# Softmax attention layer on one core: two positions of the tensor engine's order taken together

## The chip, the cores and the metric

One core of one Trainium2 chip runs the whole program in one launch. The metric is device time in microseconds (us). The core's engines are TensorE (PE in the profile; PEld is its weight load), VectorE (DVE), ScalarE (ACT), GpSimd (POOL) and SyncE (SP), which here only issues transfers. Each engine runs its own instructions in the order in which the program lists them and waits at semaphores for the others.

## The reference

Four stages follow each other, each with a residual and a layer norm: a causal softmax attention with a projection (8 batches of 1024 tokens, width 256, 16 heads of 16) and a small linear layer behind it, a linear attention with a feed-forward layer, and a mixture of experts. The change touches the first alone:

```python
att = jnp.einsum('bhqd,bhkd->bhqk', q, k) * SCALE      # q, k, v: 8 x 16 x 1024 x 16
att = jnp.where(causal, att, -jnp.inf)
att = jax.nn.softmax(att, axis=-1)
y = jnp.einsum('bhqk,bhkd->bhqd', att, v)
y = y.transpose(0, 2, 1, 3).reshape(B, T, C)
return y @ W_proj + b_proj
```

## The kernel before, in words

`softmax_layer` (from line 293) computes the first stage. A batch is walked in 48 **positions** k: 4 groups of 4 heads, and 12 pieces of the causal triangle in each (`SEGS`). At a position TensorE does this, for each of two `pair`s of heads:

- `scores(k, pair)`, called S below (line 774): the transposed scores of 128 keys against up to 512 queries, the row maxima already subtracted by two extra rows of the operand. ScalarE's `exponentials` (line 880) turns them into `probs`.
- `maxima(k + 16, pair)`, called M (line 760): plain scores of a piece that is due 16 positions later (`LM`), only to find the maxima. VectorE's `reduce` (lines 1034 and 1037) reads them.

Besides, a position has `values(k - 2)`, called V (line 794, both pairs at once: probabilities by values into `psum_o`), and at most one **unit**, called U: a transposition, a projection or part of one, from the table `UNIT_AT` (positions 1 to 44 have one). Names of units: T1, QK and V prepare the next batch; YT, P, T2, F and END finish the one before; OUT transposes attended heads; N transposes the maxima (line 733).

The widths of S, M and V go with k modulo 12. S and M of a position have 512 columns at 0 and 4 to 8, 384 at 1 and 9, 256 at 2 and 10, 128 at 3 and 11. V has the width of position k - 2.

What sets the order:

- S and M share a ring of three places in PSUM, `R` (tile `a_scores`): S(k,0), M(k,0), S(k,1), M(k,1), S(k+1,0) and so on. A product may start when the third before it has been taken out. So each S waits for VectorE's reduction of the M two products ahead of that, and each M for ScalarE's exponential of an S: M(k,1) for that of S(k,0), M(k+1,0) for that of S(k,1), S(k+1,0) for the reduction of M(k,0), S(k+1,1) for that of M(k,1).
- All units share one single place, `G` (tile `a_general`), which ScalarE or VectorE empties in `take`, at the start of the next position. The next unit waits for that.
- V(k) waits for the exponentials of position k, and where the causal edge cuts, for GpSimd's `cut`. VectorE's `copy_out` (line 1062) takes `psum_o` out at k modulo 12 = 1 and 5, behind a V.
- VectorE also does statistics (`BATCH_NORM_STATS2`, lines 1120 and 1128), the combination of maxima `together` (line 1045) at k = 8, 20, 32, 44, and `minus` (lines 1053 and 1056), which takes out N.
- SyncE's part and GpSimd's part are lists of their own, untouched.

The order of TensorE at one position is that of `turn` in `of_tensor` (line 805):

```python
scores(b, RU, k, 0)
maxima(b + (k + LM) // NK, b, RU, k + LM, 0)      # if more
values(b, RU, k - 2)
scores(b, RU, k, 1)
maxima(b + (k + LM) // NK, b, RU, k + LM, 1)      # if more
unit(batch_of(b, UNIT_AT[k]), b, U, UNIT_AT[k])   # if there is one
```

Of the kernel before, what the change touches and what calls it, by code (L numbers as in the profile page):

```python
# [292 lines left out]
def softmax_layer(nc, ctx, ident, minus_half, spot, x_rows, W_qkv, b_qkv, W_proj, b_proj, weight,  # L293
# [14 lines left out]
    NK = HG * NSEG  # L308
# [3 lines left out]
    LM = 16  # L312
# [185 lines left out]
    def kept(what, with_head, with_tail):  # L498
        if what[0] in TAIL_UNITS:
            return with_tail  # L500
        return with_head or not (what[0] in HEAD_UNITS or what == ("N", 4))
# [4 lines left out]

    def r_units(u0, with_head):
        units = {}
        for k in range(NK):
            for pair in range(2):  # L510
                units["S", k, pair] = u0 + len(units)
                if k + LM < NK or with_head:
                    units["M", k + LM, pair] = u0 + len(units)
        return units

    H_SEQ = ([("T1", i) for i in range(4)] + [("QK", i) for i in range(4)] +
# [11 lines left out]
    RU_TURN = r_units(2 * LM, True)  # L528
# [149 lines left out]
    def of_tensor(pe, prepare):  # L678
# [121 lines left out]
        def batch_of(b, what):  # L800
            if what[0] in TAIL_UNITS:
                return b - 1
            return b + 1 if what[0] in HEAD_UNITS or what == ("N", 4) else b

        def turn(b, U, RU, with_head, with_tail, prepare=None):
            for k in range(NK):
                more = k + LM < NK or with_head
                scores(b, RU, k, 0)
                if more:
                    maxima(b + (k + LM) // NK, b, RU, k + LM, 0)  # L810
                if k > 1:
                    values(b, RU, k - 2)
                elif with_tail:
                    values(b - 1, RU_TURN, NK - 2 + k)
                scores(b, RU, k, 1)
                if more:
                    maxima(b + (k + LM) // NK, b, RU, k + LM, 1)
                if k in UNIT_AT and kept(UNIT_AT[k], with_head, with_tail):
                    unit(batch_of(b, UNIT_AT[k]), b, U, UNIT_AT[k])

        def before():
            for what in H_SEQ[0:12]:
# [23 lines left out]
    def of_scalar(act, prepare):  # L846
# [52 lines left out]
        def turn(b, U, RU, with_head, with_tail, prepare=None):  # L899
            for k in range(NK):  # L900
                what = UNIT_AT.get(k - 1)
                if what and what[0] in ON_ACT and kept(what, with_head, with_tail):
                    take(b - 1 if what[0] in TAIL_UNITS else b + 1, b, U, what)
                exponentials(b, RU, k, 0)
                exponentials(b, RU, k, 1)
                if with_head and k in HEAD_APPLY:
                    head_apply(b + 1, HEAD_APPLY[k])
                if with_tail and k in TAIL_APPLY:
                    tail_apply(b - 1, *TAIL_APPLY[k])
# [112 lines left out]
    def of_vector(dve, prepare):  # L1022
# [112 lines left out]
        def turn(b, U, RU, with_head, with_tail, prepare=None):  # L1135
            for k in range(NK):
                n, mk = k % NSEG, k + LM
                more = mk < NK or with_head
                what = UNIT_AT.get(k - 1)
                if what and what[0] in ON_DVE and kept(what, with_head, with_tail):  # L1140
                    of = (b - 1 if what[0] in TAIL_UNITS else
                          b + 1 if what[0] in HEAD_UNITS or what == ("N", 4) else b)
                    take(of, b, U, what)
                if more:
                    reduce(b, b, RU, mk, 0)
                if n == 5:
                    copy_out(b, k // NSEG * 2)
                elif n == 1 and k > 1:
                    copy_out(b, k // NSEG * 2 - 1)
                elif k == 1 and with_tail:  # L1150
                    copy_out(b - 1, 2 * HG - 1)
                if n == 8 and (mk - 1 < NK or with_head):
                    together((mk - 1) // NSEG, b, RU, mk - 1)
                if with_head and k == HEAD_SUM:
                    ln_h.sum_first(dve, b + 1, chain_h)
                if with_head and k == HEAD_SUM + 1:
                    ln_h.sum_third(dve, b + 1, chain_h)
                if with_tail and k in TAIL_SUM:
                    ln_t.sum_first(dve, b - 1, chain_t)
                if with_tail and k - 1 in TAIL_SUM:  # L1160
                    ln_t.sum_third(dve, b - 1, chain_t)
                if more:
                    reduce(b, b, RU, mk, 1)
                if with_head and k in HEAD_STATS:
                    head_statistics(b + 1, HEAD_STATS[k])
                if with_head and k == HEAD_SUM:
                    ln_h.sum_second(dve, b + 1, chain_h)
                if with_tail and k in TAIL_STATS:
                    tail_statistics(b - 1, b, U, TAIL_STATS[k][0], TAIL_STATS[k][1:])
                if with_tail and k in TAIL_SUM:  # L1170
                    ln_t.sum_second(dve, b - 1, chain_t)
                if prepare is not None:
                    prepare(k)
# [1805 lines left out]
```

How the kernel before makes its waits and increments, by code:

```python
    def wait_free(self, eng, b, u):  # L76
        eng.wait_ge(self.evacuated[u % self.slots], b * self.per + self.start + u // self.slots)
# [1 line left out]
    def wait_full(self, eng, b, u):  # L79
        eng.wait_ge(self.full[u % self.slots], b * self.per + u // self.slots + 1)
# [1 line left out]
    def wait_evacuated(self, eng, b, u):  # L82
        eng.wait_ge(self.evacuated[u % self.slots], b * self.per + self.start + u // self.slots + 1)
# [1 line left out]
    def wait_evacuated_before(self, eng, b, u):  # L85
        eng.wait_ge(self.evacuated[u % self.slots], b * self.per + u // self.slots + 2)
# [12 lines left out]
    def link(self, eng, b, ins):  # L100
        self.at += 1
        ins.then_inc(self.sem, 1)
        eng.wait_ge(self.sem, b * self.per + self.at)
# [5 lines left out]
    def wait(self, eng, b):  # L109
        eng.wait_ge(self.sem, b * self.per + self.at)
# [74 lines left out]
            @block.gpsimd  # L185
            def _(pool):
                nc.gpsimd.memset(ident[:, :], 0.0).then_inc(made, 1)
                nc.gpsimd.memset(minus_half[:, :], -0.5).then_inc(made, 1)
                pool.wait_ge(made, 2)
                nc.gpsimd.affine_select(out=ident[:, :], in_=ident[:, :], compare_op=ALU.not_equal,
                                        fill=1.0, base=0, pattern=[[-1, P]],
                                        channel_multiplier=1).then_inc(made, 1)
                pool.wait_ge(made, 3)
                nc.gpsimd.iota(number[:, :], [[P, G4]], base=0, channel_multiplier=1
                               ).then_inc(made, 1)
# [470 lines left out]
        def wait_scores():  # L666
            sp.wait_ge(pv_done, B * NK + PV0)
```

## Time and profile before

| what | value |
|---|---|
| median of 3 runs | 4210.25 us (4207.5 to 4215.37) |
| the profiled execution's own time | 4209.16 us |
| its span, first to last instruction | 4207.4 us |
| busy in the span: PE, DVE, ACT, POOL | 93%, 64%, 50%, 28% |
| the stage of the change | from 103.6 us (first S) to 1325.3 us (last S) |

The profile is one execution. A row of the view of instructions in time gives start, duration, engine, source line, operation, what is written and read, and how many were merged; in brackets the idle time of the engine before it and what ended that. Durations of matmuls are longer than the distance between starts, since they overlap: S with 512 columns is shown with 0.50 us, and the next product starts 0.34 us later. The argument goes by starts.

### The profile page before, as it was taken

To read this page: it belongs to the slowest core of one execution; us is meant where nothing else is said; L and a number is where in the kernel's file an instruction comes from. 1 tells how busy PE (TensorE), PEld (TensorE's weight loads), DVE (VectorE), ACT (ScalarE), POOL (GpSimd) and SP (SyncE) were. 2 spreads that over 40 slices of the span, in tenths; PEclk is the share of its full clock that TensorE was granted. 3 is DMA by queue.
4 is the path that set the end of the run, shared out by engine and by line. 5 is a ranking of instruction groups with operands and counts; after the bars stand their busy time and mean duration, and the time that the engine had idled before them with its cause. 6 is when DMAs were issued, how large, how long until landed. Compare 5 with 4: busy or idle time off the path is not lost. (4 is left out here: it accounts for less than half of the span.)

```text
span 4207.4 us, 74610 instructions
## 1 busy us (share of the span) xinstructions
PE 3893.2 (93%) x28676; PEld 3028.3 (72%) x28676; DVE 2712.3 (64%) x7778; ACT 2115.5 (50%) x3994; POOL 1172.9 (28%) x1083
## 2 busy tenths in 40 slices
PE   4999999999999899999999999999999599999993
PEld 2444444444545788888888888888888499999992
DVE  5888888888785565555565565555555555555555
ACT  1566666666666555554455554554454333333333
POOL 3233343343333211111112111111111133333335
PEclk8899999999988999999999999999999799999996
DMA  3543544443441100000000000000001133333345
GB/s 70 99 97 57 97 92 67 87 98 61 77 110 43 36 26 21 22 21 21 20 22 22 22 19 19 16 20 10 20 20 34 52 65 65 73 69 65 65 122 173
DMA packets 177203, 230.73 MB, mean 55 GB/s; under 512 B 27388, under 2 KB 152411, under 8 KB 176848
## 3 DMA queue, kind: packets, MB, share of 16 engines
q1 hardware_dynamic: 148816, 189.53, 19.6%
q0 software_dynamic: 25728, 28.03, 4.5%
q10 hardware_dynamic: 2304, 8.39, 0.5%
q8 instruction: 228, 3.74, 0.4%
q14 instruction: 127, 1.04, 0.1%
HBM read 94.30 MB, written 87.05 MB: 43 GB/s over the span
## 5 line engine op out<-in xcount | busy, mean ns | idle before, releaser
L880 ACT ACTIVATE probs<-a_scores 128x1024 f32<-128x1024 f32 (+3 forms) x768 | 615.7, 811 | 337.7 <-PE a_scores L774 331.8
L1034 DVE CUSTOM_DVE_ANT_0 a_scores<-a_scores,mask 128x384 f32<-128x384 f32 (+3 forms) x1024 | 480.6, 514 | 101.9 <-PE a_scores L760 96.2
L774 PEld LDWEIGHTS a_scores<-q_st,k_st 50*128 50x128 f32 x1536 | 149.1, 191 | 355.4 <-issue 201.5
L273 POOL TENSOR_TENSOR l_ln_rstd<-l_ln_ve,minus_half 128x4 f32<-128x4 f32 x80 | 82.0, 1025 | 1047.5 <-DVE l_ln_ve L246 1047.1
L1842 ACT ACTIVATE l_o<-l_num,l_den 128x64 f32<-128x64 f32 x960 | 222.0, 319 | 292.6 <-DVE l_den L2328 281.1
L774 PE MATMUL a_scores<-q_st,k_st 50*128 50x512 f32 (+3 forms) x1536 | 349.9, 453 | 10.3 <-DVE mx L1034 4.0
L760 PE MATMUL a_scores<-k_st,q_st 48*128 48x512 f32 (+3 forms) x1536 | 305.9, 396 | 50.7 <-ACT probs L880 22.1
L1037 DVE TENSOR_REDUCE mx<-a_scores 128x2 f32<-128x1024 f32 x256 | 309.9, 1221 | 60.8 <-PE a_scores L760 60.1
L794 PE MATMUL a_out<-probs,v_aug 128*32 128x512 f32 (+3 forms) x3072 | 345.1, 523 | 3.4 <-POOL probs L961 3.2
L961 POOL TENSOR_SCALAR_AFFINE_SELECT probs<-probs 128x512 f32<-128x512 f32 x256 | 164.8, 645 | 518.5 <-ACT probs L880 507.3
L2664 PE MATMUL e_out<-e_weights_hi,e_hT_hi 128*128 128x256 f32 x1088 | 303.8, 279 | 0.0
L2664 PE MATMUL e_out<-e_weights_hi,e_hT_lo 128*128 128x256 f32 x1088 | 303.8, 279 | 0.0
L2664 PE MATMUL e_out<-e_weights_lo,e_hT_hi 128*128 128x256 f32 x1088 | 303.7, 279 | 0.0
L2711 ACT ACTIVATE e_to_split<-e_hidden,e_b 128x384 f32<-128x384 f32 (+1 forms) x320 | 200.0, 625 | 196.9 <-PE e_hidden L2649 189.8
L1751 PE MATMUL l_num<-l_v,l_scores_kept 128*128 128x65 f32 x2048 | 286.2, 263 | 0.0
L1751 PEld LDWEIGHTS l_num<-l_v,l_scores_kept 128*128 128x128 f32 x2048 | 271.2, 193 | 0.0
L1856 ACT ACTIVATE l_o<-l_general 128x512 f32<-128x512 f32 x256 | 152.6, 596 | 218.1 <-PE l_general L1600 199.0
L2733 POOL DMA_INDIRECT expert_sums_scratch<-e_y,e_number x136 | 221.6, 1629 | 69.6 <-issue 37.2
L2229 DVE TENSOR_TENSOR l_a<-l_general,l_a 128x512 f32<-128x512 f32 x64 | 44.3, 692 | 299.6 <-PE l_general L1559 161.2
L760 PEld LDWEIGHTS a_scores<-k_st,q_st 48*128 48x128 f32 x1536 | 154.4, 198 | 114.5 <-ACT probs L880 80.7
L2649 PE MATMUL e_hidden<-e_rT_hi,e_weights_hi 128*128 128x384 f32 (+1 forms) x640 | 233.8, 365 | 0.0
L1746 PE MATMUL l_num<-l_state,l_qT 128*128 128x130 f32 x1024 | 231.6, 308 | 0.0
(294 smaller groups left out, 10569.4 us busy)
## 6 DMA issues: line engine op xcount, KB each, us to landing
q_st<-parts SPq DMA_DIRECT2D x192, 128.0 KB, 4.5
k_st<-parts SPq DMA_DIRECT2D x192, 128.0 KB, 6.8
expert_rows_scratch<-empty_row SPq DMA_DIRECT2D x34, 520.0 KB, 9.5
l_x<-x_scratch SPq DMA_DIRECT2D x32, 512.0 KB, 3.8
e_weights<-in_L_ffn_W_dram SPq DMA_DIRECT2D x16, 1024.0 KB, 7.3
e_rows<-expert_rows_scratch SPq DMA_DIRECT2D x24, 390.0 KB
e_rows<-expert_rows_scratch SPq DMA_DIRECT2D x16, 520.0 KB
x_in<-in_L_attn_x_dram SPq DMA_DIRECT2D x8, 1024.0 KB, 5.5
```

The lines of the kernel that those rows point to most:

```text
L760: last = nc.tensor.matmul(psum_r[:, R.slot(u), h2, 0:w], q_st[rows, 2 * hg + pair, j * P:(j + 1) * P], k_st[rows, 2 * hg + pair, k0:k1], s ...
L774: last = nc.tensor.matmul(psum_r[:, R.slot(u), h2, 0:w], k_st[rows, 2 * hg + pair, i * P:(i + 1) * P], q_st[rows, 2 * hg + pair, q0:q0 + w ...
L794: last = nc.tensor.matmul(psum_o[32 * h4:32 * h4 + 32, q0 - half * HALF:HALF], v_aug[:, i, h * DV0:h * DV0 + 32], probs[:, k % 3, h4, 0:w] ...
L880: nc.scalar.activation(probs[:, k % 3, 2 * pair:2 * pair + 2, 0:w], psum_r[:, R.slot(u), :, 0:w], ACT.Exp).then_inc(R.evacuated[R.slot(u)], 1)
L1034: last = nc.vector.tensor_tensor_reduce(s, s, mask[:, HALF - w:HALF], 1.0, LEAST, ALU.add, ALU.max, out[:, h2, :])
L1037: last = nc.vector.tensor_reduce(out.rearrange("p h a -> p (h a)"), psum_r[:, R.slot(u), :, 0:w], AX.X, ALU.max)
L1746: nc.tensor.matmul(psum_n[:, NUM.slot(n), p2 * 2 * DV:(p2 + 1) * 2 * DV], qT[:, p, j * P:(j + 1) * P], state[:, p, :], start=True, stop=Fa ...
L1751: last = nc.tensor.matmul(psum_n[:, NUM.slot(n), h4 * DV:(h4 + 1) * DV], scores[:, d % 2, h2, p % 4, :], v_aug[:, j, 4 * g4 + h4, :], star ...
L1842: last = nc.scalar.activation(o[:, j % 2, head:head + DH1], psum_n[:, NUM.slot(n), h * DV:h * DV + DH1], ACT.Copy, scale=den[:, n % 2, 1, ...
L2649: last = nc.tensor.matmul(psum_h[:, HU.slot(u), 0:n * P], w1[a][:, e2, c, m * P:(m + 1) * P], rT[b][:, q % 2, c, 0:n * P], start=(k == 0), ...
L2664: last = nc.tensor.matmul(psum_y[:, s, (j - 2 * s) * D:(j - 2 * s + 1) * D], hT[a][:, q % 2, m, j * P:(j + 1) * P], w2[b][:, e2, m, :], st ...
L2733: nc.gpsimd.indirect_dma_start(out=sums_dram, out_offset=bass.IndirectOffsetOnAxis(ap=number[:, q % RING, j:j + 1], axis=0), in_=y[:, q % ...
```

## The change

Positions are taken two at a time, k even. TensorE's order for a pair of positions becomes

- S(k,0) M(k,0) S(k,1) V(k-2) M(k,1)
- S(k+1,0) M(k+1,0) U(k) V(k-1) S(k+1,1) M(k+1,1) U(k+1)

The unit of an even position moves behind the first S and M of the odd one, beside V. ScalarE and VectorE follow: at an odd position the first exponential and the first reduction now stand ahead of the `take` of the even position's unit. `r_units` is rewritten, but numbers the ring as before. No instruction is added or removed, and GpSimd's and SyncE's lists stay.

```diff
@@ turn in of_tensor
-            for k in range(NK):
-                more = k + LM < NK or with_head
+            for k in range(0, NK, 2):
+                more, of = k + LM < NK or with_head, b + (k + LM) // NK
                 scores(b, RU, k, 0)
                 if more:
-                    maxima(b + (k + LM) // NK, b, RU, k + LM, 0)
+                    maxima(of, b, RU, k + LM, 0)
+                scores(b, RU, k, 1)
                 if k > 1:
                     values(b, RU, k - 2)
                 elif with_tail:
-                    values(b - 1, RU_TURN, NK - 2 + k)
-                scores(b, RU, k, 1)
+                    values(b - 1, RU_TURN, NK - 2)
                 if more:
-                    maxima(b + (k + LM) // NK, b, RU, k + LM, 1)
+                    maxima(of, b, RU, k + LM, 1)
+                scores(b, RU, k + 1, 0)
+                if more:
+                    maxima(of, b, RU, k + 1 + LM, 0)
                 if k in UNIT_AT and kept(UNIT_AT[k], with_head, with_tail):
                     unit(batch_of(b, UNIT_AT[k]), b, U, UNIT_AT[k])
+                if k > 1:
+                    values(b, RU, k - 1)
+                elif with_tail:
+                    values(b - 1, RU_TURN, NK - 1)
+                scores(b, RU, k + 1, 1)
+                if more:
+                    maxima(of, b, RU, k + 1 + LM, 1)
+                if k + 1 in UNIT_AT and kept(UNIT_AT[k + 1], with_head, with_tail):
+                    unit(batch_of(b, UNIT_AT[k + 1]), b, U, UNIT_AT[k + 1])
@@ turn in of_scalar
                 what = UNIT_AT.get(k - 1)
+                if k % 2 == 1:
+                    exponentials(b, RU, k, 0)
                 if what and what[0] in ON_ACT and kept(what, with_head, with_tail):
                     take(b - 1 if what[0] in TAIL_UNITS else b + 1, b, U, what)
-                exponentials(b, RU, k, 0)
+                if k % 2 == 0:
+                    exponentials(b, RU, k, 0)
                 exponentials(b, RU, k, 1)
@@ turn in of_vector
                 what = UNIT_AT.get(k - 1)
+                if k % 2 == 1 and more:
+                    reduce(b, b, RU, mk, 0)
                 if what and what[0] in ON_DVE and kept(what, with_head, with_tail):
...
                     take(of, b, U, what)
-                if more:
+                if k % 2 == 0 and more:
                     reduce(b, b, RU, mk, 0)
```

TensorE at positions 6 and 7 of a batch that has a batch before it (L774 is S, L760 is M, L794 is V, L692 a unit P, L681 a unit YT). Before:

```order
L681 MATMUL a_general<-ident,y_att 128x128 x4
L774 MATMUL a_scores<-q_st,k_st 128x512 x2
L760 MATMUL a_scores<-k_st,q_st 128x512 x2
L794 MATMUL a_out<-probs,v_aug 32x512 x4
L774 MATMUL a_scores<-q_st,k_st 128x512 x2
L760 MATMUL a_scores<-k_st,q_st 128x512 x2
L692 MATMUL a_general<-w_proj,yT 128x256 x4
L774 MATMUL a_scores<-q_st,k_st 128x512 x2
L760 MATMUL a_scores<-k_st,q_st 128x512 x2
L794 MATMUL a_out<-probs,v_aug 32x512 x4
```

The same place in the changed kernel (L776 is S, L762 M, L796 V, L694 P, L683 YT):

```order
L683 MATMUL a_general<-ident,y_att 128x128 x4
L776 MATMUL a_scores<-q_st,k_st 128x512 x2
L762 MATMUL a_scores<-k_st,q_st 128x512 x2
L776 MATMUL a_scores<-q_st,k_st 128x512 x2
L796 MATMUL a_out<-probs,v_aug 32x512 x4
L762 MATMUL a_scores<-k_st,q_st 128x512 x2
L776 MATMUL a_scores<-q_st,k_st 128x512 x2
L762 MATMUL a_scores<-k_st,q_st 128x512 x2
L694 MATMUL a_general<-w_proj,yT 128x256 x4
L796 MATMUL a_out<-probs,v_aug 32x512 x4
```

V(4) went from ahead of S(6,1) to behind it, and the unit of position 6 from behind M(6,1) to behind M(7,0).

VectorE from the second reduction of position 8 on (each masked reduction is a row with the product's width and a short one that reads its result; L1120 are statistics, L1053 and L1056 take out the unit N of position 8). Before:

```order
L1034 ISA a_scores,mx<-a_scores,mask 128x512
L1034 ISA mx 128x1
L1120 BN_STATS a_ln_tail_stats<-att 128x6 x2
L1053 TENSOR_SCALAR nm_hi<-a_general 32x128
L1056 SCALAR_TENSOR_TENSOR nm_lo<-a_general,nm_hi 32x128
L1034 ISA a_scores,mx<-a_scores,mask 128x384
L1034 ISA mx 128x1
```

In the changed kernel:

```order
L1051 ISA a_scores,mx<-a_scores,mask 128x512
L1051 ISA mx 128x1
L1137 BN_STATS a_ln_tail_stats<-att 128x6 x2
L1051 ISA a_scores,mx<-a_scores,mask 128x384
L1051 ISA mx 128x1
L1051 ISA a_scores,mx<-a_scores,mask 128x384
L1051 ISA mx 128x1
L1070 TENSOR_SCALAR nm_hi<-a_general 32x128
L1073 SCALAR_TENSOR_TENSOR nm_lo<-a_general,nm_hi 32x128
```

The reduction of M(9,0), two halves of 384 columns, went ahead of the two instructions that take out N.

## Rows read from the trace of the kernel before

**Rows 1.** The page: busy time of each engine, and two of its lines in 40 slices.

```profile
PE 3893.2 (93%) x28676; PEld 3028.3 (72%) x28676; DVE 2712.3 (64%) x7778; ACT 2115.5 (50%) x3994; POOL 1172.9 (28%) x1083
...
PE   4999999999999899999999999999999599999993
...
DVE  5888888888785565555565565555555555555555
```

**Rows 2.** Windows of one batch: us, busy PE, PEld, DVE, ACT, POOL, PEclk, DMA share, GB/s.

```profile
407.00:560.00 153.00, 145.22 (x1014) 72.93 (x1014) 132.34 (x396) 103.83 (x152) 59.86 (x68) 1.00 0.44 83
```

**Rows 3.** One source line, L1053: it runs four times in a batch.

```profile
L1053 DVE TENSOR_SCALAR nm_hi<-a_general x32: 260/273/275, 99.2 to 1289.2; 32x128 fp32r<-32x128 f32 x32
```

**Rows 4.** Waits from 100 to 1200 us: total us, times, longest.

```profile
PE a_scores L760 <- ACT probs L880: 19.6, 49, 0.7
...
PE a_general L733 <- DVE mx L1045: 11.5, 14, 1.0
```

**Rows 5.** Groups by shape in one batch (560 to 714 us): busy us, mean ns | idle before.

```profile
L880 ACT ACTIVATE probs<-a_scores 128x1024 f32<-128x1024 f32 x48 | 48.8, 1024 | 14.9 <-PE a_scores L774 14.3
L1037 DVE TENSOR_REDUCE mx<-a_scores 128x2 f32<-128x1024 f32 x32 | 38.7, 1220 | 6.0 <-PE a_scores L760 6.0
```

**Rows 6.** TensorE in time, second half of position 5 and position 6 of batch 3.

```profile
573.87 0.50 PE L774 MATMUL a_scores<-q_st,k_st 50*128 50x512 f32 x2
574.42 0.49 PE L760 MATMUL a_scores<-k_st,q_st 48*128 48x512 f32 x2
574.84 0.66 PE L681 MATMUL a_general<-ident,y_att 128*128 128x128 f32 x4
575.43 0.50 PE L774 MATMUL a_scores<-q_st,k_st 50*128 50x512 f32 x2
575.77 0.39 PE L760 MATMUL a_scores<-k_st,q_st 48*128 48x512 f32 x2
576.09 1.06 PE L794 MATMUL a_out<-probs,v_aug 128*32 128x512 f32 x8
577.08 0.50 PE L774 MATMUL a_scores<-q_st,k_st 50*128 50x512 f32 x2
577.42 0.39 PE L760 MATMUL a_scores<-k_st,q_st 48*128 48x512 f32 x2
```

**Rows 7.** VectorE in time, then ScalarE, the same stretch.

```profile
575.18 0.68 DVE L1062 COPY oT<-a_out 128x512 f32<-128x512 f32 x1
575.78 1.22 DVE L1037 TENSOR_REDUCE mx<-a_scores 128x2 f32<-128x1024 f32 x1
...
576.03 1.02 ACT L880 ACTIVATE probs<-a_scores 128x1024 f32<-128x1024 f32 x1
```

**Rows 8.** VectorE in time around the taking out of N, positions 8 and 9.

```profile
587.76 0.74 DVE L1120 BATCH_NORM_STATS2 a_ln_tail_stats<-att 128x6 f32<-128x256 f32 x2
588.43 0.26 DVE L1053 TENSOR_SCALAR nm_hi<-a_general 32x128 fp32r<-32x128 f32 x1
588.72 0.28 DVE L1056 SCALAR_TENSOR_TENSOR nm_lo<-a_general,nm_hi 32x128 fp32r<-32x128 f32 x1
588.93 0.54 DVE L1034 CUSTOM_DVE_ANT_0 a_scores<-a_scores,mask 128x384 f32<-128x384 f32 x1
...
589.92 0.59 DVE L1034 CUSTOM_DVE_ANT_0 a_scores<-a_scores,mask 128x384 f32<-128x384 f32 x1
```

**Rows 9.** TensorE in time: the unit of position 9 and the product ahead of it.

```profile
588.84 0.34 PE L760 MATMUL a_scores<-k_st,q_st 48*128 48x384 f32 x2
589.11 0.70 PE L692 MATMUL a_general<-w_proj,yT 128*128 128x256 f32 x2
```

**Rows 10.** The same at positions 20 and 21: TensorE's units, and VectorE's second instruction on N.

```profile
627.46 0.41 PE L733 MATMUL a_general<-ident,mx 128*32 128x128 f32 x2 [0.94 <-DVE mx L1045]
...
629.54 0.28 DVE L1056 SCALAR_TENSOR_TENSOR nm_lo<-a_general,nm_hi 32x128 fp32r<-32x128 f32 x1
...
629.88 0.50 PE L740 MATMUL a_general<-xnT_hi,w_qkv_hi 128*128 128x512 f32 x1
```

More of the change, by code:

```diff
@@ L508, in r_units @@
         units = {}
-        for k in range(NK):
[L510 to L513, printed above, removed]
+        for k in range(0, NK, 2):
+            more = k + LM < NK or with_head
+            for at in (k, k + 1):
+                for pair in range(2):
+                    units["S", at, pair] = u0 + len(units)
+                    if more:
+                        units["M", at + LM, pair] = u0 + len(units)
         return units
@@ L805, in turn @@
         def turn(b, U, RU, with_head, with_tail, prepare=None):
-            for k in range(NK):
-                more = k + LM < NK or with_head
+            for k in range(0, NK, 2):
+                more, of = k + LM < NK or with_head, b + (k + LM) // NK
                 scores(b, RU, k, 0)
                 if more:
-                    maxima(b + (k + LM) // NK, b, RU, k + LM, 0)
+                    maxima(of, b, RU, k + LM, 0)
+                scores(b, RU, k, 1)
                 if k > 1:
@@ L813, in turn @@
                 elif with_tail:
-                    values(b - 1, RU_TURN, NK - 2 + k)
-                scores(b, RU, k, 1)
+                    values(b - 1, RU_TURN, NK - 2)
                 if more:
-                    maxima(b + (k + LM) // NK, b, RU, k + LM, 1)
+                    maxima(of, b, RU, k + LM, 1)
+                scores(b, RU, k + 1, 0)
+                if more:
+                    maxima(of, b, RU, k + 1 + LM, 0)
                 if k in UNIT_AT and kept(UNIT_AT[k], with_head, with_tail):
                     unit(batch_of(b, UNIT_AT[k]), b, U, UNIT_AT[k])
+                if k > 1:
[3 more added lines that the diff above has]
+                scores(b, RU, k + 1, 1)
+                if more:
+                    maxima(of, b, RU, k + 1 + LM, 1)
+                if k + 1 in UNIT_AT and kept(UNIT_AT[k + 1], with_head, with_tail):
+                    unit(batch_of(b, UNIT_AT[k + 1]), b, U, UNIT_AT[k + 1])
         def before():
```

## The prediction

> **What bounds the kernel now.** I read the page first: TensorE is busy 93% of the span and in tenths of 9 almost everywhere, VectorE 8 tenths only in the first third, which is the stage of the change [rows 1]. Everything outside that stage keeps its instructions and order, so the change is worth what it does to the 8 batches. Their length comes from a line that runs four times a batch: 31 intervals from 99.2 to 1289.2 us, so (1289.2 - 99.2) / 31 x 4 = 153.5 us a batch [rows 3]. The window of one batch shows TensorE 145.2 of 153 us busy, VectorE 132.3, ScalarE 103.8, at a granted clock of 1.00 [rows 2]. So TensorE has at most some 8 us of idle in a batch by the records, and VectorE has 20 us of slack, 13%: it is close enough behind to decide wherever its work is not spread evenly.
>
> The waits say where TensorE's idle is. M waits for exponentials (19.6 us) and the unit N for VectorE's combined maxima (11.5 us), in 1100 us, which are 7.2 batches: 2.7 and 1.6 us a batch [rows 4].
>
> **Prices, from starts.** S to M takes 0.34 us, M to V 0.32, a V of 512 columns 0.99, S to M again 0.34 [rows 6]. A full exponential takes 1.02 and a full reduction 1.22 [rows 5]. The reduction of M(5,1), started on TensorE at 574.42, ran from 575.78 to 577.00, because the copy of `psum_o` (575.18) went first; S(6,1), which needs its place, started at 577.08 [rows 6, 7].
>
> **What the change leaves alone.** No engine gets more work, the ring's numbering is the same, and SP's and POOL's lists stay, so no transfer is passed by anything. Only distances move. Before, every S and M had a V or a unit on either side: the lead of each hand-over was nearly the same. Now there are runs S M S and M S M without anything between, and runs with V and U together.
>
> **Part 1, gain: the M behind exponentials.** At an odd position M(k,1) waited for the exponential of S(k,0), which stood behind ScalarE's taking out of a unit. S(5,1) to M(5,1) took 0.55 instead of 0.34 [rows 6]: 0.21 lost. Now this exponential goes first and a unit lies in between, so it goes. Seven odd positions have this form. But M(k+1,0) now comes after S M S V M S and needs both exponentials of the even position. Behind a unit that ScalarE takes out they begin 0.60 after S(k,0), as at position 6 (576.03 - 575.43), and end at 0.60 + 2 x 1.02 = 2.64 [rows 6, 7]. With a V of 256 columns (some 0.57) the TensorE work is 0.34 + 0.32 + 0.34 + 0.57 + 0.32 + 0.34 = 2.23: a new wait of 0.4. So part of the gain is given back at the even positions with a narrow V. Ends: nothing, and all of the 2.7 us a batch [rows 4]. I take 1.1 us a batch, nearer to the lower end because the give-back is seen to be of the size of the gain.
>
> **Part 2, loss: V behind an S that waits for VectorE.** At even k, S(k,1) needs the reduction of M(k-1,1). Before, V(k-2) lay between and was done while VectorE finished. At position 6 V(4) ran from 576.09 to 577.08, and the reduction ended at 577.00: the wait cost nothing [rows 6, 7]. In the new order TensorE comes to S(6,1) at 576.09, waits until 577.05 and only then does V(4): M(6,1) can start at 577.05 + 0.34 + 0.99 = 578.4, before 577.42. That is 1.0 us. Nor is the reduction earlier: at position 5 the copy waits for V(3), which now stands behind unit 4. The form needs a light unit or none at k-1 (a heavy one, such as P, covers the wait); that is k = 2, 6, 14, 30 with the copy ahead of the reduction, and 0, 32, 34, 44, 46 without. Walking the starts of these stretches in the same way gives 0.8 for positions 0 to 3, 1.2 for 4 to 7, 0.6 for 12 to 17, 0.3 for 28 to 31, nothing sure for 44 to 47: 2.9 us a batch. In 12 to 17 this already holds the gain of part 1. Ends: 0 and twice as much.
>
> **Part 3, loss: the unit's single place.** A unit of an even position is now followed by the next one after only V S M, and VectorE takes it out one reduction later. At position 8 VectorE has no idle ahead of it: statistics 587.76, N taken out 588.43 to 589.00, and unit 9 starts at 589.11, right at the end of the M before it (588.84 + 0.27) [rows 8, 9]. Now two halves of 384 columns go first; from 588.93 to 589.92 they take 0.99 us [rows 8]. N's place is free at 590.0, and unit 9 waits for it 0.9 us. At position 21 the same: taken out at 629.54 + 0.28 = 629.82, unit at 629.88 [rows 10], so another 1.0. Here the gain of the later N is contained: N waited 0.94 for the maxima [rows 10] and now waits less, but the next unit is held by the later taking out. Position 33 by the same walk 0.4; position 39, a QK behind OUT with a reduction of 128 columns and statistics ahead of it, 0.7. Together 3.0 us a batch. Ends: 0, if VectorE is earlier there for another reason, and 4.5.
>
> **The sum.** 2.9 + 3.0 - 1.1 = 4.8 us a batch. The first and the last batch lack part of the units, so I count 7: 34 us. On the profiled execution's own time of 4209.2 this is 4243; the median of the runs shown is 1 us higher and nothing else. The granted clock was 1.00 in the middle batches [rows 2], and I count no change of it.
>
> **The rivals.** *Faster: the waits for exponentials and maxima go and VectorE's slack pays for the rest.* The Trainium skill (same page, Optimization Strategy) advises one to find the gaps of the chosen engine and let what ends them start sooner; this change does that for TensorE. If it holds, half of the 19.6 us (the odd positions) and the 11.5 us go [rows 4]: 4209 - 21 = 4188. For it: the waits are real, and VectorE has 13% slack. Against: at 575.78 and 587.76 VectorE runs without idle just where the new order asks more of it. It decides if reductions at even positions end before the second S comes.
>
> *No change.* What one pair loses, the next regains, since later waits are shortened by VectorE having caught up: within 8 us of 4210. For it: the total of work is the same. Against: the stalls are followed by positions that had no wait to give back (10, 11).
>
> *Much slower.* The late reductions pile up: each holds the next exponentials and S too, and more of the units with a single place are held. Then the upper ends of parts 2 and 3 hold and nothing is gained: (5.8 + 4.5) x 7 = 72, so 4281. Against: VectorE's load of 87% lets it catch up at positions of 128 and 256 columns, and where ScalarE takes a unit out, V, S and M (0.99 + 0.34 + 0.32 = 1.65 us) mostly cover that [rows 6]. The Trainium skill has a rule on this side (Perfetto Trace Analysis, Optimizing Tensor Performance, Matmuls): groups of matmuls should rotate through different PSUM banks, so that taking one out lies beside the next. By that rule each of some 20 odd units would be held; at 0.9 each (an estimate with unit 9's price) that would be 126 us and a time of 4335. The trace of before bears it out for VectorE's units only.
>
> *The change does not do what it says* is no case: the order above shows it done on three engines.
>
> **How the numbers follow.** A measurement tells about 0.2%, 8.4 us, from no change. My forecast (a loss of 12 to 55 us around 4243) has 0.60, faster 0.15, no change 0.14, much slower 0.11. All of the first and the last are slower by over 0.2%, and one in seven of the no-change case (0.02) could fall out above: slower 0.73, same 0.12, faster 0.15. The range takes in my forecast, the no-change case and a part of the faster one, and on the other side all but the full pile-up: 4194 to 4270. That leaves out some 0.1 on either side.
>
> **What would show it.** In the new profile a batch, by the same line's 31 intervals, should be 158.3 us instead of 153.5; waits of L776 (S) for VectorE's maxima should have grown, waits of L762 (M) for exponentials should have fallen to half or less; the units of positions 9 and 21 should wait for the second instruction on N by some 0.9 us; and V(4) should start after S(6,1). I am wrong if the batch is 153 us or less, or if the time is lost at M behind exponentials instead.

## The result, and the profile after

The changed kernel takes 4291.7 us (median of 4 runs, 4283.0 to 4309.8) against 4208.9 of the kernel before beside it: a ratio of 1.0204, 95% interval 1.0182 to 1.0226. It is 83 us slower; 34 were forecast, and the time lies above the range. The profiled execution has a span of 4281.3 us.

The page of the changed kernel, as [rows 1], with the line of the granted clock:

```profile
PE 3918.0 (92%) x28676; PEld 3051.8 (71%) x28676; DVE 2699.9 (63%) x7778; ACT 2105.4 (49%) x3994; POOL 1172.1 (27%) x1083
...
PEclk8889999899898999999999999999999799999996
```

The work is that of before: instruction counts and busy times of VectorE, ScalarE and GpSimd hardly move. TensorE's busy time rises by 25 us with the same 28676 matmuls, so some took longer in the records. The line that runs four times a batch, as [rows 3]:

```profile
L1070 DVE TENSOR_SCALAR nm_hi<-a_general x32: 273/274/279, 102.1 to 1363.3; 32x128 fp32r<-32x128 f32 x32
```

(1363.3 - 102.1) / 31 x 4 = 162.7 us a batch: 9.2 more than before, 71 us in the 31 intervals. So the loss is in this stage, as expected. Windows of the changed kernel, columns as in [rows 2]: one as long as that of before, one at positions 2 and 3 of batch 3, one from position 46 of batch 3 to position 3 of batch 4.

```profile
407.00:560.00 153.00, 139.54 (x958) 71.36 (x958) 123.24 (x375) 97.47 (x146) 55.59 (x64) 0.96 0.45 84
595.00:604.00 9.00, 8.10 (x45) 3.94 (x46) 5.50 (x26) 3.14 (x7) 2.91 (x4) 0.62 0.97 186
750.00:768.00 18.00, 17.77 (x98) 7.82 (x98) 11.05 (x44) 9.15 (x15) 6.71 (x8) 0.53 0.86 148
```

The granted clock is 0.96 where it was 1.00, and the fall lies in short stretches that come back in each batch, in which it is close to 0.50: the level of 1.2 GHz instead of 2.4. There a value product of 512 columns takes almost twice as long. TensorE at positions 2 and 3 of batch 3, changed kernel (start, duration, and in brackets the idle time before and what ended it):

```profile
596.49 0.49 PE L776 MATMUL a_scores<-q_st,k_st 50*128 50x256 f32 x2 [0.90 <-DVE mxb L1051]
596.92 1.93 PE L796 MATMUL a_out<-probs,v_aug 128*32 128x512 f32 x8
598.78 0.58 PE L762 MATMUL a_scores<-k_st,q_st 48*128 48x256 f32 x2
```

V(0) takes 598.78 - 596.92 = 1.86 us from start to start instead of 0.99 [rows 6]. Ahead of it stands the wait that part 2 of the forecast describes.

At position 6 that part can be read as forecast: S(6,1) waits for VectorE, and V(4) starts behind it.

```profile
608.85 0.49 PE L776 MATMUL a_scores<-q_st,k_st 50*128 50x512 f32 x2
609.22 0.50 PE L762 MATMUL a_scores<-k_st,q_st 48*128 48x512 f32 x2
610.33 0.50 PE L776 MATMUL a_scores<-q_st,k_st 50*128 50x512 f32 x2 [0.60 <-DVE mx L1054]
610.76 1.06 PE L796 MATMUL a_out<-probs,v_aug 128*32 128x512 f32 x8
611.76 0.50 PE L762 MATMUL a_scores<-k_st,q_st 48*128 48x512 f32 x2
```

The reduction it waits for, and the copy ahead of that, as [rows 7]:

```profile
608.46 0.68 DVE L1079 COPY oT<-a_out 128x512 f32<-128x512 f32 x1
609.05 1.22 DVE L1054 TENSOR_REDUCE mx<-a_scores 128x2 f32<-128x1024 f32 x1
```

It ends at 610.27, and S(6,1) starts at 610.33. From S(6,0) to M(6,1) are 2.91 us; before they were 1.99 [rows 6]. At positions 8 and 9 part 3 can be read. VectorE's taking out of N, and the unit of position 9, as [rows 8, 9]:

```profile
622.70 0.55 DVE L1051 CUSTOM_DVE_ANT_0 a_scores<-a_scores,mask 128x384 f32<-128x384 f32 x1
...
623.99 0.28 DVE L1073 SCALAR_TENSOR_TENSOR nm_lo<-a_general,nm_hi 32x128 fp32r<-32x128 f32 x1
```

```profile
622.62 0.35 PE L762 MATMUL a_scores<-k_st,q_st 48*128 48x384 f32 x2
624.32 0.91 PE L694 MATMUL a_general<-w_proj,yT 128*128 128x256 f32 x3 [1.35 <-DVE nm_lo L1073]
```

TensorE idles 1.35 us for the second instruction on N; 0.9 was worked out. Waits of TensorE in the same 1100 us as [rows 4]:

```profile
PE a_scores L776 <- DVE mx L1054: 12.3, 29, 0.7
PE a_scores L776 <- DVE mxb L1051: 10.4, 25, 0.9
...
PE a_scores L776 <- DVE mx L1051: 8.6, 18, 0.8
PE a_general L742 <- DVE nm_lo L1073: 8.5, 7, 1.3
PE a_general L694 <- DVE nm_lo L1073: 8.2, 6, 1.4
PE a_scores L762 <- ACT probs L894: 7.7, 24, 0.7
...
PE a_general L735 <- DVE mx L1062: 0.2, 1, 0.2
```

The two waits at which the change aims did fall: M behind exponentials from 19.6 to 7.7 us, N behind the maxima from 11.5 to 0.2 [rows 4]. Two others grew. S behind reductions takes 31 us. In the kernel before it was 6, in the same view:

```profile
PE a_scores L774 <- DVE mx L1034: 3.7, 10, 1.1
...
PE a_scores L774 <- DVE mxb L1034: 1.6, 6, 0.5
...
PE a_scores L774 <- DVE mx L1037: 0.8, 2, 0.5
```

And the units behind VectorE's taking out of the unit before them wait some 49 us in sum, where they waited 6.

**A table by pairs.** The starts of S(k,0) show each pair of positions by itself. The table gives the mean over batches 1 to 6 from one pair's first S to the next pair's, in us, from the traces of the kernels before and after and of eight of the experiments below (their labels without e_), one execution each.

```
pair   before   after  v_only  u_only  thin_old  thin_new  fill   thin_fill  before_fill  n_first
46      4.22    5.94    4.62    4.69     4.30      4.48    6.58     5.40        4.90       4.60
 0      4.93    5.52    4.67    4.94     4.88      4.67    5.51     5.50        5.50       5.41
 2      4.72    7.76    8.12    5.30     4.72      7.24    4.92     4.92        4.56       6.20
 4      5.39    5.40    7.32    5.55     5.56      6.84    5.55     5.40        5.39       5.96
 6      8.50    9.30   10.12    9.36     9.29     10.06    9.30     8.49        8.49       9.45
 8      7.11    8.07    7.07    8.07     8.07      7.12    8.07     7.12        7.11       7.07
10      5.90    5.71    5.90    6.43     5.71      5.90    5.71     5.90        5.89       6.16
12      6.18    6.68    6.07    6.50     6.12      6.68    6.89     6.88        6.42       6.45
14      5.93    7.78    7.89    5.68     5.97      7.07    5.42     5.63        5.17       6.91
16      8.14    7.78    8.30    8.93     8.94      7.91    7.53     7.29        7.74       9.08
18      7.88    8.03    8.11    8.97     8.02      7.97    8.03     7.81        7.83       8.82
20      7.37    7.72    7.37    7.73     7.70      7.37    7.71     7.36        7.37       6.71
22      6.38    6.66    6.28    6.65     6.66      6.28    6.66     6.53        6.28       6.82
24      7.57    7.12    7.14    7.39     7.13      7.15    7.12     7.18        7.15       7.13
26      5.64    5.74    5.65    6.13     5.75      5.63    5.75     5.64        5.63       5.75
28      5.39    5.22    5.39    5.48     5.23      5.40    5.23     5.39        5.40       5.23
30      5.96    6.31    6.43    6.66     6.29      5.95    6.30     5.96        5.96       6.29
32      6.01    6.85    6.21    6.44     6.85      6.01    6.85     6.01        6.01       6.21
34      7.33    7.20    8.03    7.77     7.72      7.33    7.20     7.33        7.33       7.83
36      7.79    7.72    7.79    7.98     7.72      7.79    7.72     7.79        7.79       7.72
38      5.85    6.32    5.88    6.32     6.32      5.87    6.32     5.86        5.87       6.32
40      7.63    7.39    7.61    7.49     7.38      7.61    7.39     7.64        7.61       7.39
42      6.83    6.93    7.25    7.56     6.95      6.83    6.94     6.82        6.84       6.94
44      6.31    5.76    6.22    5.54     5.75      6.30    5.76     6.32        6.30       6.21
sum   154.96  164.90  165.42  163.53   159.00    161.46  160.43   156.17      154.53     162.67
```

Of the 9.9 us that a batch lost, 7.7 are at the pairs 46, 0, 2, 12 and 14, called thin stretches below: there the products are narrow or the units light or missing.

The means of the kernel before hold two falls of the clock of its own. Pair 24 takes 7.13 us in five of the six batches and 9.78 in batch 1; in batch 6 the pairs 12, 14 and 16 take 6.68, 8.08 and 10.10, in the other five 6.08, 5.50 and 7.75. So at pair 24 the new order (7.12) gains nothing, though the means say 0.45, and at pair 16 (7.78) neither.

### The profile page after: what moved, and what is told of

Read it like the earlier page. It is cut to its first block and busy times, and to the rows that moved or that the text cites. A ratio compares the mean times of both kernels' runs of the same rounds, so it can differ in the third digit from the quotient of the medians.

```text
span 4281.3 us, 74610 instructions
## 1 busy us (share of the span) xinstructions
PE 3918.0 (92%) x28676; PEld 3051.8 (71%) x28676; DVE 2699.9 (63%) x7778; ACT 2105.4 (49%) x3994; POOL 1172.1 (27%) x1083
## 5 line engine op out<-in xcount | busy, mean ns | idle before, releaser
L894 ACT ACTIVATE probs<-a_scores 128x1024 f32<-128x1024 f32 (+3 forms) x768 | 606.1, 811 | 396.1 <-PE a_scores L776 391.4
L796 PE MATMUL a_out<-probs,v_aug 128*32 128x512 f32 (+3 forms) x3072 | 374.0, 554 | 2.2 <-POOL probs L978 2.2
L776 PE MATMUL a_scores<-q_st,k_st 50*128 50x512 f32 (+3 forms) x1536 | 332.3, 432 | 45.3 <-DVE mxb L1051 15.0
L762 PE MATMUL a_scores<-k_st,q_st 48*128 48x512 f32 (+3 forms) x1536 | 317.2, 419 | 31.7 <-ACT probs L894 9.1
L776 PEld LDWEIGHTS a_scores<-q_st,k_st 50*128 50x128 f32 x1536 | 154.9, 199 | 263.2 <-issue 100.3
L762 PEld LDWEIGHTS a_scores<-k_st,q_st 48*128 48x128 f32 x1536 | 158.7, 203 | 229.0 <-ACT probs L894 140.2
```

Of the source, the lines that this page charges most:

```text
L762: last = nc.tensor.matmul(psum_r[:, R.slot(u), h2, 0:w], q_st[rows, 2 * hg + pair, j * P:(j + 1) * P], k_st[rows, 2 * hg + pair, k0:k1], s ...
L776: last = nc.tensor.matmul(psum_r[:, R.slot(u), h2, 0:w], k_st[rows, 2 * hg + pair, i * P:(i + 1) * P], q_st[rows, 2 * hg + pair, q0:q0 + w ...
L796: last = nc.tensor.matmul(psum_o[32 * h4:32 * h4 + 32, q0 - half * HALF:HALF], v_aug[:, i, h * DV0:h * DV0 + 32], probs[:, k % 3, h4, 0:w] ...
L894: nc.scalar.activation(probs[:, k % 3, 2 * pair:2 * pair + 2, 0:w], psum_r[:, R.slot(u), :, 0:w], ACT.Exp).then_inc(R.evacuated[R.slot(u)], 1)
```

## The experiments

Two theories stood against each other. **A**: the order makes TensorE wait in the thin stretches, the granted clock falls there, and this is most of what the forecast missed. **B or C**: the waits themselves are larger than worked out, because one place for the units (B) or late reductions (C) drag what follows; the lower clock is a by-product. The expectations call a stretch in which the granted clock is near 0.50 a half-clock stretch; below it is a low stretch.

All experiments are one kernel with sets of even positions: `V_LATE` (V behind the second S), `U_LATE` (unit in the odd position) and `TAKE_LATE` (ScalarE's and VectorE's taking behind the first exponential and reduction). All empty is the order of before, all full is the change.

```diff
+            for k in range(NK):
+                late_v = k % 2 == 0 and k in V_LATE
                 scores(b, RU, k, 0)
                 if more:
                     maxima(of, b, RU, k + LM, 0)
+                if k % 2 == 1 and k - 1 in U_LATE and has(k - 1):
+                    do_unit(k - 1)
+                if not late_v:
+                    do_values(k)
                 scores(b, RU, k, 1)
+                if late_v:
+                    do_values(k)
                 if more:
                     maxima(of, b, RU, k + LM, 1)
+                if has(k) and not (k % 2 == 0 and k in U_LATE):
+                    do_unit(k)
```

**V moved alone.**

```diff
+    V_LATE = list(range(0, 48, 2))
+    U_LATE = TAKE_LATE = []
```

> V alone is moved (behind the second S at even positions); the units and the orders of ScalarE and VectorE are those of before. Theory A (V behind an S that waits for VectorE starves TensorE in the thin stretches, positions 46 to 3 and 12 to 15, and the granted clock falls there): most of the loss is here, about +50 us against before, clock in the middle batches 0.95, pair 2-3 near 7 us instead of 4.7, pairs 8-9 and 38-39 as before (7.11 and 5.85). Theory B (the units' single place is the cause, and it drags the rest): under +15 us, clock 1.00.

Measured: ratio 1.0203 (1.0173 to 1.0234), 4294.5 us. Pair 2 takes 8.12, pair 14 7.89, pairs 8 and 38 are as before. The granted clock between 250 and 1180 us is 0.93, where the changed kernel has 0.94. The places and the clock are those of theory A, but its size is missed: 85 us over before instead of 50, so V alone costs as much as the whole change. Of the batches 2 to 5 the one with the least of the low level (batch 3, 3.4 us) takes 159.1 us, the others (20.5 to 27.3 us) 164.7 to 166.2.

**The unit moved alone**, with its taking.

```diff
+    V_LATE = []
+    U_LATE = TAKE_LATE = list(range(0, 48, 2))
```

> The unit of the even position alone is moved, with ScalarE's and VectorE's late taking; V stays where it was before. Theory A: pairs 8-9, 20-21, 32-33 and 38-39 lose 0.3 to 1.0 each, the thin stretches nothing: +10 to +20 us, clock 1.00. Theory B: +50 us or more and a clock of 0.95 in the middle batches.

Measured: ratio 1.0160 (1.0134 to 1.0186), 4279.7 us, 67 us over before. Theory A gave at most 20 and missed; the time is the one that theory B gave (50 or more), but not its clock. The clock over the same stretch is 0.98, and pair 2 takes 5.30, so this loss is mostly not the clock's: batches 1 and 5 have no low stretch and take 161.9 and 161.8 us, 8.5 more than the kernel before with none (153.4). It is spread: pairs 10, 12, 16, 18, 26, 30, 34 and 42 lose 0.3 to 1.1 each, besides 8, 20, 32 and 38. Nor is it the units' place that waits most, but M behind exponentials. From 250 to 1180 us, this run first and then before (the changed kernel has 5.8 us there):

```profile
PE a_scores L768 <- ACT probs L904: 51.9, 114, 0.7
```

```profile
PE a_scores L760 <- ACT probs L880: 14.5, 34, 0.7
```

Here S, M, S, M stand in a row without V or unit between, so M(k+1,0) comes sooner behind S(k,1), whose exponential it needs: 86 of the 114 waits and 35 of the 52 us are at that M. The next S comes sooner behind its reduction too, and the trace at pair 6 shows it waiting:

```profile
439.49 0.40 PE L768 MATMUL a_scores<-k_st,q_st 48*128 48x512 f32 x2
440.27 0.51 PE L782 MATMUL a_scores<-q_st,k_st 50*128 50x512 f32 x2 [0.38 <-DVE mx L1065]
440.77 0.50 PE L768 MATMUL a_scores<-k_st,q_st 48*128 48x512 f32 x2
441.20 1.99 PE L700 MATMUL a_general<-w_proj,yT 128*128 128x256 f32 x8
```

So the two moves are not two separate costs: 2.0% and 1.6% alone make 2.0% together. In the changed kernel V stands between S(k,1) and M(k+1,0), and that wait is small. The wait that part 1 is about is shortened by the two moves together and made longer by the unit's alone.

**The thin stretches in the old order, and the complement.**

```diff
+    V_LATE = U_LATE = TAKE_LATE = [all even positions but 46, 0, 2, 12, 14]
```

> The changed kernel with the order of before at the pairs that start at 46, 0, 2, 12 and 14. If the loss is local to the pairs: the pairs left in the new order lose 2.3 us a batch in sum, so about +16 us against before (4225), and the clock in the middle batches is back at 1.00. If the clock or the lateness is spread by the other pairs, the clock stays under 0.98 and the time is over 4240.

Measured: ratio 1.0071 (1.0045 to 1.0097), 4244.1 us, a clock of 0.98 from 250 to 1180. That is about 30 us over before where local loss gave 16. Of the pairs left in the new order, 6 to 10 and 18 to 44 take what they took in the changed kernel (but 34, which fell to the low level in two batches and took 8.77 there). Pair 16 takes 8.94 instead of 7.78: in three batches most of that is the clock (9.45, 10.17 and 10.15 us), in the three others it takes 7.81 to 8.04. The two batches without a low stretch take 156.9 us, 3.5 over before where 2.3 were expected. The result lies between the two branches of the expectation: the loss is not local, since the clock still falls, also at pair 34, where it did not in the changed kernel.

```diff
+    V_LATE = U_LATE = TAKE_LATE = [46, 0, 2, 12, 14]
```

> The complement: the order of before, with the new order only at the pairs that start at 46, 0, 2, 12 and 14. Local loss: 7.7 us a batch, seven batches, so about +54 us (4263), clock 0.95 in the middle batches. If the loss needs the other pairs too: under +25 us.

Measured: ratio 1.0112 (1.0084 to 1.0140), 4261.3 us, clock 0.94 from 250 to 1180: the first branch, with 47 us over before where 54 were expected. This trace holds the clearest comparison of the study. Pair 2 is run with the same instructions in each batch. In three of the batches 1 to 6 it takes 5.62 us, in three 8.86. Two windows of it, batch 2 and batch 3 (columns as in [rows 2]):

```profile
417.30:422.90 5.60, 4.71 (x41) 2.42 (x40) 4.71 (x23) 3.13 (x7) 2.32 (x4) 1.00 1.01 163
573.70:582.60 8.90, 8.00 (x43) 3.72 (x42) 5.30 (x25) 3.17 (x7) 2.89 (x4) 0.58 1.05 181
```

TensorE in batch 2, second S of position 2 to the next product:

```profile
418.78 0.38 PE L782 MATMUL a_scores<-q_st,k_st 50*128 50x256 f32 x2 [0.89 <-DVE mxb L1062]
419.09 1.06 PE L802 MATMUL a_out<-probs,v_aug 128*32 128x512 f32 x8
420.09 0.39 PE L768 MATMUL a_scores<-k_st,q_st 48*128 48x256 f32 x2
```

and the same in batch 3:

```profile
575.23 0.58 PE L782 MATMUL a_scores<-q_st,k_st 50*128 50x256 f32 x2 [0.90 <-DVE mxb L1062]
575.75 1.93 PE L802 MATMUL a_out<-probs,v_aug 128*32 128x512 f32 x8
577.61 0.58 PE L768 MATMUL a_scores<-k_st,q_st 48*128 48x256 f32 x2
```

The wait for VectorE is 0.9 us in both. What differs is the clock: V takes 1.00 us in one and 1.86 in the other. So of the 4.1 us that pair 2 lost in those batches against 4.72, the order took 0.9 and the clock 3.2. Whole batches show the same, batch 2 and batch 4 from S(0,0) to S(0,0):

```profile
412.61:569.07 156.46, 148.27 (x1017) 74.64 (x1017) 132.38 (x396) 103.89 (x153) 60.14 (x69) 0.98 0.42 81
733.08:903.82 170.74, 163.26 (x1016) 80.85 (x1017) 133.14 (x396) 104.39 (x153) 60.13 (x69) 0.87 0.41 76
```

One order takes 156.5 us with 6.8 us at the low level and 170.7 with 44.4.

**Idle time of TensorE filled.** The strongest test of theory A gives TensorE more work and expects less time.

```diff
+    FILL_EMPTY = [46, 47, 0]; FILL_UNIT = [1, 12, 13]
...
+                if k in FILL_EMPTY and (k > 0 or b > 0):
+                    if k == 46:
+                        G.wait_evacuated(pe, b, max(U.values()))
+                    for j in range(4):
+                        nc.tensor.transpose(psum_g[:, j * P:(j + 1) * P], ident[:, :], ident[:, :])
```

Its output in the units' free place is never read. It was put into the complement (`e_thin_new`):

> e_thin_new with idle time of TensorE filled: four transpositions of the identity into the free place of the units behind positions 46, 47 and 0, and the transpositions of the units of positions 1, 12 and 13 done twice (six times 0.59 us a batch, 3.5 us more work). Theory A (the granted clock is most of the loss; the order alone costs about 1.5 us a batch there): no half-clock stretch at positions 2 and 14 of the middle batches, pair 2-3 near 5.6 us in every batch instead of 5.6 to 8.9, batches of 156 to 159 us, so the time falls by 10 to 30 us against e_thin_new although there is more work. Theory C (late reductions pile up, the clock is a by-product): pairs 2-3 stay at 7 or more and the time rises by up to 25 us.

Measured: ratio 1.0044 (1.0026 to 1.0061), 4225.8 us, so 0.7% or about 28 us less than without the filling. No low stretch is left in batches 2 to 5, and they take 155.5 us, a little less than the 156.4 to 156.9 of the three batches of `e_thin_new` in which the clock nearly held (6.8 us low). Pair 2 takes 4.92 us in every batch, less than 5.6, but pair 0 ahead of it takes 5.50 instead of 4.67: the two together are 10.4 against 10.3, so the wait has only moved. Into the changed kernel:

> The changed kernel with the same filling (3.5 us more TensorE work a batch). Theory A: stretches at half the clock fall from 23 us a batch to under 8, batches from 165 to 159 to 161 us, time 4245 to 4265. Theory C: time 4290 to 4315.

Measured: ratio 1.0125 (1.0095 to 1.0155), 4256.8 us against 4291.7. The windows from 250 to 1180 us of the changed kernel with filling and of before:

```profile
250.00:1180.00 930.00, 846.87 (x6042) 441.46 (x6041) 764.61 (x2312) 595.50 (x880) 341.70 (x389) 0.99 0.45 83
```

```profile
250.00:1180.00 930.00, 884.49 (x6100) 445.09 (x6097) 796.77 (x2377) 625.02 (x913) 360.97 (x408) 0.99 0.45 83
```

The clock is as before, and still a batch takes 160.4 us. It holds a rest of the clock's part: in every second batch the level is low for 3.4 us at position 46, and pair 46 takes 7.35 us instead of 5.81. The batches without that take 159.7: this is the order's own price, with the filling in it. What the filling costs where nothing is to be mended shows in the kernel before:

> The kernel before, its order untouched, with the same filling as e_thin_fill (six times 0.59 us more TensorE work a batch). It prices the filling itself. Theory A (the filling helped e_thin_new and e_fill through the clock alone): here it only costs, 1 to 3 us a batch, 4210 to 4230, clock 1.00 in the middle batches as before. If the filling is a gain here too (under 4200), it does something else than keep the clock.

Measured: ratio 0.9996 (0.9981 to 1.0010), 4207.3 us: nothing that can be told, a little under the 4210 to 4230 that were expected. By the traces it adds 1.1 us to a batch at full clock (154.5 against 153.4 us) and saves the low stretches that the kernel before has in batches 1 and 6 itself. It is no gain by itself, so in the two others it worked through the clock. Theory C, as the cause of what the forecast missed, falls, and not only because pair 2 is short with the filling (VectorE could have caught up meanwhile): in `e_thin_new`, without filling, the same wait of 0.9 us is followed by a short pair 2 and 4 wherever the clock holds.

**VectorE takes out N first.**

```diff
+    TAKE_LATE = [all even positions but 8, 20, 32, 44]
```

> The changed kernel, but VectorE takes out the unit N (positions 8, 20, 32, 44) ahead of the first reduction of the odd position, as before the change. If part 3 of the forecast names the wait rightly, pairs 8-9, 20-21 and 32-33 fall from 8.07, 7.72 and 6.85 to about 7.2, 7.3 and 6.1: 2 us a batch, 15 us in all (4277), the clock stretches unchanged. If the units' single place is not what ends the wait of unit 9, they stay.

Measured: ratio 1.0177 (1.0148 to 1.0206), 4279.4 us, 12 us under the changed kernel; the intervals overlap, so the times alone do not show a gain. The trace does at its place. Pairs 8, 20 and 32 take 7.07, 6.71 and 6.21 instead of 8.07, 7.72 and 6.85: 2.6 us a batch, a little more than expected. The unit of position 9 waits 0.37 us instead of 1.35:

```profile
630.74 1.99 PE L700 MATMUL a_general<-w_proj,yT 128*128 128x256 f32 x8 [0.37 <-DVE nm_lo L1084]
```

So part 3 names this wait rightly. But the pairs behind gave back 1.7 of the 2.6 us at full clock: 10, 34 and 44 lost 0.45 to 0.63 each and 22 lost 0.16. Pairs 16 and 18 lost 1.3 and 0.8 more, to the clock: the low level moved there from pairs 46 to 2 and in part from 14. That the stretches stay as they were had been expected, and they did not. Pair 20, at 6.71, is the only pair of this kind that is clearly better than before (7.37).

**Two versions picked from the pairs.**

```diff
+    V_LATE = [10, 24, 28, 34, 36, 40]
+    U_LATE = TAKE_LATE = V_LATE + [44]
```

> The order of before, the new one only where the traces show a gain: pairs 10, 24, 28, 34, 36, 40 whole, and at 44 the unit alone. From the pairs in the traces: 0.19 + 0.45 + 0.17 + 0.14 + 0.07 + 0.24 + about 0.5 (0.77 less what 46 gives back) = 1.8 us a batch, so 12 us under before (0.3%), clock 1.00. If the gains were bought from the neighbours or the clock falls at 46 to 3, no gain or a loss.

Measured: ratio 0.9998 (0.9977 to 1.0019), no change. In its trace pair 34 takes 7.67 instead of 7.20, pair 10 6.11 instead of 5.71, both more than in the kernel before: their gain in the changed kernel came with the pair ahead, which had lost. Pair 46 gives 0.34 of pair 44's 0.61 back. The 0.45 expected at pair 24 were the low stretch of batch 1 in the kernel before and no gain of the order. Batches without a low stretch take 153.0 and 153.5 us, those of before 153.4. It is the second branch of the expectation, gains bought from neighbours, and a mean that was misread.

```diff
+    V_LATE = [12, 14, 20, 24, 28, 36, 40]
+    U_LATE = V_LATE + [44]
+    TAKE_LATE = [12, 14, 24, 28, 36, 40, 44]; FILL_UNIT = [12, 13]
```

> A version picked from the pairs of all traces: the new order at 12, 14, 20, 24, 28, 36, 40 (at 20 with VectorE taking out N first), at 44 the unit alone, the units of 12 and 13 done twice, the rest as before. From the pairs: +0.7 (12), -0.3 (14), -0.9 (16), -0.5 (20 and 22), -0.4 (24), -0.2 (28), +0.1 (30), -0.1 (36), -0.2 (40), -0.3 (44 and 46): 2.1 us a batch, 15 us under before (4190 to 4195), no half-clock stretch in the middle batches. If the gains are bought from the neighbours, within 0.2% of before.

Measured: ratio 0.9981 (0.9966 to 0.9997), 4203.3 us. It is the fastest version of the study: 0.2% under the kernel before, or 8 us by the ratio (3 by the medians), with an interval that reaches to 1 us; 15 were expected. Most of the rest was never there: the expected gains at 14, 16 and 24 were taken against means with the low stretches of the kernel before. Batches without a low stretch take 153.0 us, 0.4 less than before. Pair 16 (7.39 against 7.75 at full clock) and pair 44 (5.68) kept a gain, pair 20 did not (7.37). And the low level was expected to be gone but comes for 3.4 us in batches 2, 4 and 6, at pair 14.

## Why the prediction was wrong

**The direction and, in sum, the waits were right.** In batches without a low stretch and with the filling in both kernels, the changed one takes 159.7 and the one before 154.5 us: 5.2 us, where 4.8 were forecast. In runs that is 4256.8 against 4207.3, or 50 us where 34 were forecast; the spans of the two profiled executions differ by 40, the two ratios by 54 give or take 14. A part of the sum is luck, since its terms were off both ways. The pairs below compare the same two runs.

- *Part 1, the M behind exponentials.* The wait fell as said, 19.6 to 7.7 us. The gain by pairs (10, 24, 34, 36, 40) is 0.6 us, not 1.1, and the half of it at pairs 10 and 34 is borrowed (`e_gainers`).
- *Part 2, V behind an S that waits.* At full clock positions 0 to 3 lose 0.4 (forecast 0.8), 4 to 7 1.0 (1.2), 12 to 17 0.5 (0.6), 28 to 31 0.2 (0.3): 2.0 instead of 2.9. The place at position 6 came out as worked, S(6,1) right at the end of its reduction and M(6,1) 0.9 us later. That V is the cause by itself was too simple: the unit's move alone costs pair 6 0.9 as well.
- *Part 3, the units' single place.* Pairs 8, 20 and 22, 32, 38 lose 0.96, 0.72, 0.84 and 0.45: 3.0, as forecast, with 32 larger and 20 and 38 smaller than said. `e_n_first` shows the cause for the N of 8, 20 and 32. That N itself waits less (11.5 to 0.2 us) may have a second reason beside the order, the last point of this document.
- *"Nothing sure for 44 to 47"* left out 0.4: pair 44 gains 0.5 and pair 46 loses 0.9 where the clock holds (5.81 against 4.90). Pairs 18, 26 and 42 lose another 0.4 that no part named.

**The step that failed** is "I count no change of it", of the granted clock. It was read at 1.00 in one middle batch and taken as given, although part 2 itself puts new waits where TensorE has little to do. In the changed kernel the records show the low level for 17 to 26 us of each batch 2 to 5, 20 on average, between positions 46 and 3 and between 13 and 16, where before they showed none (the 23 in the expectation of `e_fill` are too many). The filling takes 35 us off (4291.7 to 4256.8; 33 give or take 16 by the ratios). So the 83 us are about 50 of order and 33 of clock.

The kernel before had the price in its own trace. Windows of two of its batches:

```profile
867.00:1020.00 153.00, 145.20 (x1016) 73.03 (x1014) 132.42 (x395) 103.73 (x152) 59.97 (x68) 1.00 0.46 84
1020.00:1180.00 160.00, 154.38 (x1026) 77.67 (x1022) 133.30 (x399) 105.25 (x154) 61.05 (x69) 0.94 0.43 75
```

The second is the same work: 159.2 us from one S(0,0) to the next instead of 153.3, with 20.5 us at the low level, so 0.29 us lost for each. By that price 20 us would cost 5.8 a batch, 41 us in 7. The price is not the same everywhere: at pair 2 of `e_thin_new` 3.2 us were lost for 7.5, or 0.43 for each. The comparison of these two batches was missing from the working, and they show too that the order of before is itself close to such a fall.

The rivals: "faster" named waits that did go, but VectorE's slack did not pay for the others. "No change" is excluded by the interval. "Much slower" gave 4281, near the measured time, by the wrong road: a pile-up of reductions, which the batches of `e_thin_new` and the two fillings exclude as the main cause. Both pieces of advice that the prediction takes from the Trainium skill are of the page Perfetto Trace Analysis. The one on rotating groups through banks is borne out only for units that VectorE takes out: all of TensorE's waits ahead of units in those 1100 us are for VectorE, 49 us in 7.2 batches, or 7 a batch where the 4335 us of the prediction need 18.

The Trainium skill (TensorE: Matmul & The Clock Gate, A second HAM failure mode: psum-queue depth-cycling) tells of a kernel whose TensorE idles briefly between groups of matmuls while it cycles through PSUM, and whose clock swings for that. The traces here agree: in `e_thin_new` the level falls at 575.1 us, at position 2 of batch 3, and in the 23 us ahead of that no idle time is longer than 0.9 us.

**What stays open.** The same instructions fell to the low level in three batches of `e_thin_new` and not in three others, with the same wait of 0.9 us at position 2. What tips it was not found; the length of an idle time alone does not, since in the kernel before TensorE idles 0.94 us ahead of N at position 20 [rows 10] and the clock stays. Nor is it known why `e_u_only`, whose waits are longer in sum, keeps the clock nearly up.

## What to carry to other kernels

An order that only moves waits can cost clock beside the waits (here 33 us beside 50, at single pairs more than the wait itself). Look for stretches of the kernel before in which the granted clock was low, price one by comparing two equal iterations, and put a bound for such stretches into the range where the change adds idle time and TensorE's work is thin; `e_u_only` shows that they need not come. Moving one of two fillers (values, units) between hand-overs takes the cover from the other's neighbours, so gains of single pairs in one trace do not add up when they are picked alone. Means over iterations should be taken from iterations with the same clock: a low stretch of the kernel before looked like a gain of the new order at three pairs. A cheap insurance is redundant work in the thinnest places: six groups of four transpositions a batch cost nothing measurable here and bring back 0.8% where the clock was falling.

## What the runs showed of the hardware

- A V of 512 columns takes 1.00 us from start to start at the high level and 1.86 at the low one; the wait ahead of it, 0.9 us, is the same in both.
- More TensorE work made the program faster: 3.5 us of added transpositions a batch took 0.7% off `e_thin_new` and 0.8% off the changed kernel.
- One order, the same instructions: a batch of `e_thin_new` takes 156.5 us with 6.8 us at the low level and 170.7 with 44.4.
- The combination of maxima (L1045), a VectorE instruction of 0.17 us, takes 1.09 to 1.10 seven times in the kernel before, and each time a GpSimd instruction on `parts` (L938, 1.27 us) is running; it ends 0.03 us after that one. Six times it takes 0.61 to 0.62, and then GpSimd's L951 is running. In the 19 others no GpSimd instruction runs beside it. In the changed kernel GpSimd's instruction on `parts` (L955 there) is running ahead of its start only once, and there it takes 1.10. That the one holds the other up is not tested, but it fits all 32, and it is a part of the 11.5 us for which N waited before [rows 4].
